# Second attention of a small language-model tower: router logits as extra columns of the value and output projections, and a new order of the turn

## What is computed

```python
h = token + position + type embedding, layer norm
h = h + single_head_causal_attention(layernorm(h))
h = h + soft_mixture_of_64_experts(layernorm(h))      # slots; combined by a softmax over 1024 slots
h = h + attention_12_heads(layernorm(h))              # rope, softmax, w_proj, b_proj
x = layernorm(h)
logits = x @ router_w                                 # [4096, 8]
gate, index = max(softmax(logits)), argmax(logits)    # top 1 of 8 experts, at most 512 tokens each
h = h + gate * expert[index](x)
```

## Time and profile before

| what | value |
|---|---|
| time of 3 runs, median (lowest to highest) | 1368.09 us (1367.55 to 1370.77) |
| the profiled execution: its own time | 1371.76 us |
| its span, first to last instruction | 1370.1 us |
| mean granted clock of TensorE | 0.986 |
| PE, weight loads, DVE, ACT, POOL busy | 96%, 85%, 71%, 69%, 18% of the span |
| share of the chain that ended last: PE, ACT, DVE | 60%, 8%, 3% |

### The profile page before, as it was taken

One profiled execution on the slowest core, in us unless ns is written; L12 is line 12 of the kernel. 1 busy time (PEld: TensorE's weight loads), 2 busy tenths in 40 slices (PEclk: granted clock), 3 DMA queues, 4 the chain that ended last, 5 costly groups with the idle time before them and its releaser, 6 DMA issues.

```text
span 1370.1 us, 29508 instructions
## 1 busy us (share of the span) xinstructions
PE 1309.8 (96%) x8890; PEld 1169.0 (85%) x8890; DVE 976.6 (71%) x2984; ACT 948.7 (69%) x2360; POOL 252.3 (18%) x284
## 2 busy tenths in 40 slices
PE   8789999999999999999999999899999999979997
PEld 6578888888889988998899898788888889868986
DVE  7988888557787777777777774588888888732341
ACT  1478888888766666666666664488888888835552
POOL 5332110000111111111111110012122122121335
PEclk9999999999999999999999999999999999988999
DMA  7144444457666666666666666444554547115542
GB/s 204 43 151 162 157 160 150 154 191 236 196 203 188 204 189 200 191 203 188 203 194 199 191 186 214 139 151 145 155 163 142 150 143 219 33 36 141 129 98 23
DMA packets 179747, 219.99 MB, mean 161 GB/s; under 512 B 23460, under 2 KB 146570, under 8 KB 179648
## 3 DMA queue, kind: packets, MB, share of 16 engines
q1 hardware_dynamic: 146256, 178.61, 42.6%
q10 hardware_dynamic: 25712, 33.19, 7.3%
q0 software_dynamic: 7680, 6.95, 2.6%
HBM read 141.31 MB, written 79.90 MB: 161 GB/s over the span
## 4 chain that ended last, share of the span: by engine, by line
PE 60%; ACT 8%; DVE 3%; issue 2%; DMA 1%; POOL 0%; POOLq 0%; SPq 0%; ACTq 0%; DVEq 0%
PE bank L115 25%; PE bank L1354 22%; ACT probs L1853 5%; PE bank L1729 3%; PE bank L1766 2%; PE bank L91 2%; DVE head_neg_max L1963 1%; PE bank L94 1%; PE bank L1774 1%; ACT probsT L1872 1%; PE bank L1808 1%; PE bank L1828 1%; PE bank L1751 1%; ACT headsT_kq L1877 1%; PE bank L122 1%
## 5 line engine op out<-in xcount | busy, mean ns | idle before, releaser
L1354 PE MATMUL bank<-e_w,e_h_full 128*128 128x192 f32 x1920 | 324.9, 326 | 0.4
L1354 PEld LDWEIGHTS bank<-e_w,e_h_full 128*128 128x128 f32 x1920 | 310.6, 190 | 1.7 <-ACT e_h_full L1435 1.3
L1435 ACT ACTIVATE e_h_full<-bank,e_b 128x512 f32<-128x512 f32 x240 | 165.2, 689 | 155.5 <-PE bank L115 155.4
L1290 POOL TENSOR_TENSOR e_ln_rstd<-e_ln_var_eps,minus_half 128x4 f32<-128x4 f32 x62 | 62.4, 1006 | 437.1 <-DVE e_ln_var_eps L1486 437.1
L1853 ACT ACTIVATE probs<-bank,head_neg_max 128x128 f32<-128x128 f32 x384 | 134.6, 391 | 7.8 <-DVE head_neg_max L1963 5.8
L1493 DVE TENSOR_SCALAR e_rows<-e_slot_sums,e_ln_mean_var,e_ln_rstd 128x192 f32<-128x192 f32 x248 | 77.5, 376 | 77.5 <-POOL e_ln_rstd L1290 77.5
L1396 ACT ACTIVATE e_x_full<-bank,e_ln_shift,e_ln_gain 128x512 f32<-128x512 f32 x124 | 76.5, 667 | 40.7 <-issue 36.7
L1103 PE MATMUL bank<-x,dispatch_weights 128*128 128x193 f32 x512 | 95.9, 329 | 5.6 <-ACT slot_stage L948 4.8
L115 PE MATMUL bank<-e_x_hi,e_w1hi 128*128 128x512 f32 x216 | 95.5, 442 | 2.5 <-PEq L551 1.4
L1729 PE MATMUL bank<-slot_outputs_then_w_part,combineT 128*128 128x193 f32 x512 | 94.3, 337 | 2.4 <-ACT combineT L1845 2.1
L1729 PEld LDWEIGHTS bank<-slot_outputs_then_w_part,combineT 128*128 128x128 f32 x512 | 84.8, 192 | 8.9 <-issue 8.2
(11 more groups left out here) (290 smaller groups left out, 3100.3 us busy)
## 6 DMA issues: line engine op xcount, KB each, us to landing
slot_sums<-slot_stage SPq DMA_DIRECT2D x64, 386.0 KB, 3.2
e_slot_sums<-slot_sums SPq DMA_DIRECT2D x64, 386.0 KB, 3.6
slot_outputs<-e_stage ACTq DMA_DIRECT2D x64, 384.0 KB, 3.6
slot_outputs_then_w_part<-slot_outputs SPq DMA_DIRECT2D x30, 768.0 KB, 4.9
e_w<-in_w SPq DMA_DIRECT2D x64, 288.0 KB, 3.0
slot_logits<-kept_logits SPq DMA_DIRECT2D x32, 512.0 KB, 3.0
slot_logits<-slot_logits SPq DMA_DIRECT2D x32, 512.0 KB, 3.4
e_w1raw<-in_w SPq DMA_DIRECT2D x80, 192.0 KB, 2.7
```

The costliest lines, as they stand in the source:

```text
L1290: pool.tensor_tensor(rs[u][:], ve[u][:], half[:], ALU.pow).then_inc(rstd_ready, 1)
L1354: last = pe.matmul(y, hf[:, k, js], w2s[u][:, k, :], start=k == 0, stop=k == MT - 1)
L1435: act.activation(hf[:, m, :], hbank(u, m), act_fn, bias=b1s[:, m, ds(n, 1)]).then_inc(acted, 1)
```

## The change

In words:

1. The router matrix is centred over the features (`Rc`), rounded into two parts and appended as 8 columns to the value weights; and Wproj times `Rc` is appended as 8 columns to the output projection. The values' matmuls give 200 columns instead of 192, and so does the output projection. ACT scales the 8 extra value columns by the token's standard deviation of the layer norm (`std4`, a new power on POOL) and puts them beside `h`, whose rows become 200 wide (`h_wide`); the residual sum of p then adds all 200 columns, and its last 8 are the logits without the scale of the fifth layer norm, which goes into the exponential. The transposes of x5 (L1751), their copy on ACT (L1860) and the router matmul are gone, and the router's stages begin a turn earlier. The pipeline has one turn less.
2. The probabilities are turned by thirds, each third as soon as its exponentials are there.
3. The score maxima are four reductions of one bank each, at the end of DVE's turn for q, ahead of the split, instead of two at the start of the following turn.
4. ACT copies the values of a, behind the exponentials, instead of those of q at the end of the turn; the inverse sums are turned into bank 3, ahead of the scores; the residual sum of p stands behind the last rotary step; POOL issues the first scatter, both powers, then the second scatter.
5. At the start, Y(0) and Y(1) follow each other in turn 0, the exponential for Y(1) stands ahead of the rounding of x4T(0), and the spare matmuls of turns 0 and 1 go from 10 and 10 to 6 ahead of the last piece of Y(0) and 3 in turn 1. The two small matrix products of the centred router are made there, and five more DMAs load their operands ahead of the stage.

The diff, cut to its core:

```diff
-        T["h"] = al.sb("h_all", [P, NB, D])
+        T["h_wide"] = al.sb("h_all_and_logits", [P, NB, D + NE1])
+        T["h"] = T["h_wide"][:, :, 0:D]
...
+        sp.dma_start(self.WpT[:, 0, :], ins["WprojT"][0:P]).then_inc(self.WpT_in, 16)
+        sp.dma_start(self.WpT[0:DR, 1, :], ins["WprojT"][P:D]).then_inc(self.WpT_in, 16)
+        for c, rows, of in ((0, slice(0, P), slice(0, P)), (1, slice(0, DR), slice(P, D)), (1, slice(DR, P), slice(P, D))):
+            sp.dma_start(self.R[rows, c, :], ins["router"][of]).then_inc(self.R_in, 16)
...
-            for t in range(NB + 6):
+            for t in range(NB + 5):
                 turn(t, t % 2, batch(t + 1), batch(t), batch(t - 1), batch(t - 2), batch(t - 3),
-                     pair(5, t), pair(6, t), pair(7, t))
+                     pair(4, t), pair(5, t), pair(6, t))
```

PE:

```diff
+                def outputs_of(y, u):
+                    pe.wait_ge(ys_in[u], 16 * (y // 2 + 1))
+                    pe.wait_ge(S["C_exp"], y + 1)
+                    past(pe, S["h2_ready"], y)
+                    if y > 1:
+                        pe.wait_ge(S["x4_split"], y)
+                    for c in range(NC):
+                        if y < 2 and c == NC - 1:
+                            keep_busy(pe, T, bank[:, 6, :], 6 if y == 0 else 0)
+                            pe.wait_ge(early.ys_last_in[u], 16)
...
+                            outputs_of(0, 0)
+                            sum_router()
+                            outputs_of(1, 1)
+                        elif y > 1:
+                            outputs_of(y, u)
...
-                    if r is not None:
-                        bank7_free(pe, a, r, z)
-                        pe.wait_ge(S["x5_ready"], 2 * r + 2)
-                        for j in range(2):
-                            for k in range(2):
-                                last = pe.transpose(bank[:, 7, (2 * j + k) * P:(2 * j + k + 1) * P],
-                                                    x5[r % 3][:, j, TAG + k * DR:TAG + k * DR + P], ident[:])
-                        last.then_inc(S["x5T_done"], 1)
...
-                        pe.wait_ge(S["S_exp"], 4 * a + 4)
                         for k in range(3):
+                            pe.wait_ge(S["S_exp"], 4 * a + 2 + k)
...
-                    if r is not None:
-                        pe.wait_ge(S["x5T_took"], r + 1)
-                        for j in range(2):
-                            last = matmuls(pe, bank[:, 7, j * P:(j + 1) * P],
-                                           [(x5T[:, j, 0, :], rw0[:]), (x5T[:, j, 1, :], rw1[:])])
-                        last.then_inc(S["router_done"], 1)
-                    if t < 2:
-                        keep_busy(pe, T, bank[:, 6, :], 10)
+                    if t == 1:
+                        keep_busy(pe, T, bank[:, 6, :], 3)
...
-                        heads_of(bank[:, 3, 0:D], slice(2 * D, 3 * D), "v_done")
+                        heads_of(bank[:, 3, 0:D + NE1], slice(2 * D, 3 * D + NE1), "v_done")
+                    if a is not None:
+                        past(pe, S["v_took"], min(a + 1, NB))
+                        past(pe, S["einvT_took"], a)
+                        pe.wait_ge(S["einv_ready"], a + 1)
+                        for g in range(2):
+                            last = pe.transpose(bank[:, 3, (2 + g) * P:(3 + g) * P], einv_wide[:, g, :], ident[:])
+                        last.then_inc(S["einvT_done"], 1)
```

ACT:

```diff
+                def take_values(a, u):
...
+                    act.activation(T["h_wide"][:, a, D:], bank[:, 3, D:D + NE1], ACT.Copy,
+                                   scale=std4[:, a % 4:a % 4 + 1])
+                    by_halves = vs[u][:].rearrange("p (i b) (e d) -> p i (b e) d", b=2, e=2)
+                    act.activation(by_halves[:, :, 0:4:3, :],
+                                   bank[:, 3, 0:D].rearrange("p (i b d) -> p i b d", b=2, d=HD), ACT.Copy
+                                   ).then_inc(S["v_took"], 1)
...
-                            act.wait_ge(S["head_max"], 2 * a + s // 2 + 1)
+                            act.wait_ge(S["head_max"], 4 * a + s + 1)
...
-                    if r is not None:
-                        act.wait_ge(S["x5T_done"], r + 1)
-                        act.activation(x5T[:].rearrange("p j k t -> p (j k t)"), bank[:, 7, :], ACT.Copy
-                                       ).then_inc(S["x5T_took"], 1)
+                        take_values(a, u)
...
+                            last = act.activation(lex[:, j, :], lx[:, j, :], ACT.Exp, scale=rs5[:, c:c + 1])
```

DVE:

```diff
-                    if a is not None:
-                        past(dve, S["S_exp"], 4 * a)
-                        for k in range(2):
-                            dve.wait_ge(S["S_done"], 4 * a + 2 * k + 2)
-                            dve.tensor_reduce(nmx[:, 2 * k:2 * k + 2, :], bank[:, 4 + 2 * k:6 + 2 * k, 0:3 * P]
-                                              .rearrange("p s (g n) -> p s g n", g=3), AX_X, ALU.max,
-                                              negate=True).then_inc(S["head_max"], 1)
...
-                        dve.tensor_tensor(h[:, p, :], projected, h[:, p, :], ALU.add).then_inc(S["h3_ready"], 1)
                     if q is not None:
...
+                    if p is not None:
+                        dve.wait_ge(S["p_done"], p + 1)
+                        wide = T["h_wide"][:, p, :]
+                        dve.tensor_tensor(wide, projected, wide, ALU.add).then_inc(S["h3_ready"], 1)
...
                     if r is not None:
                         read_logits(r)
+                    if q is not None:
+                        past(dve, S["S_exp"], 4 * q)
+                        for k in range(4):
+                            dve.wait_ge(S["S_done"], 4 * q + k + 1)
+                            dve.tensor_reduce(nmx[:, k, :], bank[:, 4 + k, 0:3 * P].rearrange("p (g n) -> p g n", g=3),
+                                              AX_X, ALU.max, negate=True).then_inc(S["head_max"], 1)
                     if y is not None:
                         dve.wait_ge(S["x4_hi_ready"], y + 1)
                         past(dve, S["v_done"], y)
                         dve.tensor_tensor(x4lo[:], x4T[:, 0:P], x4hi[:, 0:P].bitcast(F32), ALU.subtract)
```

More of the change, by code:

```diff
@@ L1708, in _, with sum_router, project_router @@
             def _(pe):
+                def sum_router():
+                    pe.wait_ge(early.R_in, 48)
+                    pe.wait_ge(S["ones_table"], 1)
+                    matmuls(pe, R_sums, [(ones[:], early.R[:, 0, :]), (ones[0:DR], early.R[0:DR, 1, :])]
+                            ).then_inc(S["R_summed"], 1)
+                def project_router():
+                    pe.wait_ge(early.WpT_in, 32)
+                    pe.wait_ge(S["R_centred"], 1)
+                    for g in range(2):
+                        gs = slice(g * P, (g + 1) * P)
+                        last = matmuls(pe, WpR[:, g, :], [(early.WpT[:, 0, gs], Rc[:, 0, :]),
+                                                          (early.WpT[0:DR, 1, gs], Rc[0:DR, 1, :])])
+                    last.then_inc(S["WpR_done"], 1)
+                def outputs_of(y, u):
[8 more added lines that the diff above has]
+                            pe.wait_ge(early.ys_last_in[u], 16)
+                        last = pe.matmul(bank[:, 0, 0:D + 1], cT[:, c, :], ysb[u][:, c, :],
+                                         start=c == 0, stop=c == NC - 1)
+                    last.then_inc(S["Y_done"], 1)
                 def heads_of(o, c, done):
@@ L1715, in turn @@
                     if t >= NB + 2:
-                        keep_busy(pe, T, bank[:, 3, :], 6)
+                        keep_busy(pe, T, bank[:, 0, :], 6)
                     if y is not None:
@@ L1720, in turn @@
                             pe.wait_ge(S["ones_set"], 2)
-                        pe.wait_ge(ys_in[u], 16 * (y // 2 + 1))
-                        pe.wait_ge(S["C_exp"], y + 1)
-                        past(pe, S["h2_ready"], y)
-                        past(pe, S["x4_split"], y)
-                        for c in range(NC):
-                            if y < 2 and c == NC - 1:
-                                pe.wait_ge(early.ys_last_in[u], 16)
-                            last = pe.matmul(bank[:, 0, 0:D + 1], cT[:, c, :], ysb[u][:, c, :],
-                                             start=c == 0, stop=c == NC - 1)
-                        last.then_inc(S["Y_done"], 1)
+                            outputs_of(0, 0)
[3 more added lines that the diff above has]
+                            outputs_of(y, u)
                     if q is not None:
                         if q == 0:
+                            project_router()
                             pe.wait_ge(S["W_split"], 1)
@@ L1813, in turn @@
                         past(pe, S["qk_took"], min(t, NB))
-                        pe.wait_ge(S["einv_ready"], a + 1)
-                        for g in range(2):
```

(20 more changed lines are left out.)

158 lines of the change are left out of this document (91 added, 67 removed).

## The result

Before 1367.82 us, after **1459.11 us** (medians of 4 runs each; after 1455.45 to 1461.22): ratio 1.0663, 95% interval 1.0642 to 1.0683. The profiled execution of after took 1461.22 us with a span of 1459.5, 89.5 us more than that of before, and the mean granted clock is 0.952 instead of 0.986. The direction was forecast; the size was not, and not even the range of 1375 to 1411 held it.

The account below looks back on a forecast made before the run. PE was taken to set the pace (301 of 309 us busy), with the change closing a loop through DVE's split: +40.5 us for 30 turns, -5 at the start, -9 at the end, about 1394 us; range 1375 to 1411.

Parts of the forecast that it names:

- The loop: Each steady turn: S, four maxima, split and next Y form one line, 11.76 us against 10.41, +40.5 us for 30 turns.
- PE's wait for x4: Ahead of x4's transposes: PE comes first and waits about 0.4 us in one kind of turn, 0.8 in the other.
- What is removed hides: Each pair of turns: 0.42 + 0.97 us of router work and about 0.8 of exponential waits go, none on the new line.
- The sum: Whole kernel, Y at 2.60 us: 40.5 - 5 - 9 = +26.5 us, giving 1394 us.
- Rival 1: Clock falls in PE's gap ahead of Y: Y takes 4.25 instead of 2.60 us, kernel 1444 us; chance 0.08.
- The power ahead of x4 meets no scatter: POOL's power before x4 in each turn: not held up, since the first scatter is issued by the turn's start.
- Start: Before the steady turns: Y(1) follows at once, Y(2) at 870.5 instead of 875.84, -5 us; ends 0 and -7.
- Y(0) "as before": At the stage's start: Y(0) done at 856.4, unchanged, because it waits for the last slots.
- the forecast of 861.6 for the queries: At the start: Y(1) from 857.5 takes 2.6 us, x4's turning, rounding and split add 1.5; then 8.9 to Y(2).
- End: From the last turn to the load of the rows, 38.8 us before: -9 us in all; ends -4 and -12.
- The other two terms: At the end: -3 us up to S of the last batch, -3 from S to the last residual sum.
- Rival 3: Steady turns: Y never waits for the split, PE stays the bound, turn about 9.4 us, kernel 1324 us; chance 0.06.

Follow-up runs that it names:

- kernel 6: The changed kernel with three spare matmuls in PE's gap ahead of Y, results not read: 1407.62 us, ratio 1.0295.
- kernel 7: The changed kernel with eight spare matmuls in PE's gap ahead of Y and both scatters at the start of POOL's turn: 1408.1 us, ratio 1.03.
- kernel 3: The kernel before with only the maxima moved: four single-bank maxima put ahead of the split: 1415.4 us, ratio 1.0327.
- experiment 5: The changed kernel with the split ahead of the maxima and the small router products' operands loaded late (SP and ACT queues): 1350.49 us, ratio 0.9878.
- kernel 9: The changed kernel with the split ahead of the four maxima, a rerun of kernel 1 in another group: 1350.31 us, ratio 0.9852.
- kernel 10: Rerun of experiment 5: kernel 9 plus the small router products' operands loaded late: 1349.74 us, ratio 0.9846.
- kernel 8: The kernel before with four single-bank maxima right behind the split and probabilities turned by thirds, router work unchanged: 1361.69 us, ratio 0.9949.
- kernel 4: The changed kernel with both scatters of a pair issued at the start of POOL's turn: 1437.7 us, ratio 1.0479.
- kernel 1: The changed kernel with one edit, DVE's split of x4T ahead of the four maxima: 1354.98 us, ratio 0.9883.
- kernel 2: The changed kernel with eight spare matmuls behind the heads' outputs, in PE's gap ahead of Y: 1413.78 us, ratio 1.0313.

## Why the prediction was wrong, step by step

- **The loop: right.** 11.76 us was forecast, and with the clock held up the turn is 11.80 (kernels 6 and 7). Its terms hold in the trace: a maximum of 384 columns takes 0.55 us (0.56), S to the first takes 1.04 (1.02), from there to the split 1.87 (1.92), the split 0.54 (0.55), the hop to Y 0.11 (0.07): S to Y 3.56 (3.56). PE's wait for x4 is 0.27 us, shorter than the 0.4 to 0.8 that was said. 30 x (11.80 - 10.41) = +41.7 of the 96.7 us. The waits for exponentials went and bought nothing, as said under "What is removed hides".
- **"The clock falls in the gap ahead of Y ... Chance 0.08": this is the step that failed.** The sum had Y at 2.60 us in each turn, that is a clock that stays up; it was down in Y in all 30 turns, 30 x (4.27 - 2.60) = +50 us. Rival 1 had the mechanism and the price (4.25); with it the forecast would have been 1444. Two things made it look unlikely. The gap was sized as 1.6 to 1.8 us and measured 2.08. Behind the start of S, give PE 1.25 us to the heads' outputs and 0.59 for them, 1.84 in all, and 3.56 - 1.84 = 1.72 is the gap that kernel 3 has; but the inverse sums inside this 1.25 had moved ahead of S in this very change, so PE was done 1.47 us after S began (1064.08 to 1064.96 + 0.59). With the forecast's own gap, in kernel 3, the clock fell in 4 turns of 30, so the size may have mattered; as said there, it is not shown. And one row with PE at 9% for a microsecond was held against the row of Y(1), where the clock did fall. The first was a single short lull, the second the only row that had the shape of the new turn. The Trainium skill, "TensorE: Matmul & The Clock Gate", section "A second HAM failure mode: psum-queue depth-cycling", spoke for the fall: it has short waits between groups of matmuls, repeated in each iteration, as enough to make the clock swing. The trace of after agrees, 30 turns of 30 at 1.2 GHz in Y; kernel 6, with waits of 1.36 us in each turn and no fall, shows that such waits do not always do it.
- **The scatters: not in the sum.** "The power ahead of x4 meets no scatter" holds, but the second scatter runs beside S, and in after each of the thirteen turns with one has 0.41 us more ahead of the first maximum: +5 us. 41.7 + 50 + 5.3 = 97.0, against 96.7 measured.
- **Start: -5 forecast, +1.3 measured.** Y(0) "as before" was wrong: its last piece starts at 858.32, not 855.77, 1.1 of it from the experts' stage and 1.5 from the slower store (experiment 5). Of that the five DMAs are 0.6 us at most, and kernels 9 and 10 show nothing of it in the whole. Y(1) did take 2.60 us at full clock, from 860.14. Then came what the forecast of 861.6 for the queries left out: PE stood 1.44 us ahead of the router's small products, and these took 1.25. The queries started at 865.72, and Y(2) was last in a line of 11.4 us from there, not 8.9; its gap was 2.73. Of the 2.5 us more, 1.5 lie behind the end of x4 (870.70): the three spare matmuls of turn 1 stood ahead of its transposes, with the clock at 0.50 from 867 to 873 us, and the values started at 872.48. Of the rest, 0.65 is DVE's first rotary step, which stood in DVE's list behind the combine logits of the next batch (865.93 + 1.22), and 0.4 is the values, 1.16 at the low clock instead of 0.75.
- **End: -9 forecast, -7.4 measured.** From the last residual sum to the logits are 1.44 us (1308.11 to 1309.55) instead of 5.2: -3.8 for the -3 said. The other two terms together gave -3.6, not -6.
- **Rival 3, PE stays the bound at turns of 9.4**, was a picture of what the change could do in another order. With the split first the turn is 9.97 us (kernel 9, 28 turns from 885.21 to 1164.28), and PE is busy 265 of 274 us. That leaves 0.33 us of waits a turn; the rest above 9.4 is work that the sum of rival 3 had taken out too freely.

## What to carry to other kernels

Where a change makes the bounding engine wait for another in every turn, ask two questions beyond the length of the loop. How long is the gap in rows of the new order, with every item that used to fill it looked up again? And at which clock does the engine come out of it: if one row of the trace shows the fall after a similar gap, price it on every turn and give it a real chance. And when an early result (here the maxima) and the release of a shared bank (here the split) stand in one list, the release goes first: the same four reductions cost 3.3% ahead of it (kernel 3), and together with the thirds gained 0.5% behind it (kernel 8).

## What was not expected of the hardware

- **TensorE's clock, by gap.** Gaps of the weight loads ahead of Y, repeated in each turn: 2.08 and 2.50 us, low in 30 of 30 turns; 2.08 in all, in 19 of 30; 1.72, in 4 of 30, eight turns apart; 1.36, in none after Y(2). The lengths of the turns differ as well, and no run changed one and held the other, so this list is no rule of the gap. A fall cost 1.67 us, during Y only. Where falls repeat they keep a beat: 13.65 us in after, whose turns are of two lengths (13.5 and 13.9), 95.6 us in kernel 3. The cheap cure (three spare matmuls, kernel 6) gave back 50 us of the 91 by its ratio (1.0663 - 1.0295). What keeps the clock up in one turn of kernel 4 and not in the next, with equal gaps, is open.
- **With an indirect DMA of POOL issued beside S, DVE's first maximum started 0.41 us later** in all such turns of three runs (after, kernels 1 and 2) and, but for one turn with 0.06, in none of four others (kernels 5, 6, 9 and 10), kernel 9 being the same program as kernel 1. Kernel 4, in the group of kernels 1 and 2, has the scatters elsewhere and no delay. Which part of the scatter does it, and what differs between the runs, was not tried.
- **The start differs between runs of one program too:** Y(2) took 2.59 us in kernel 1 and 4.01 in kernel 9.
